# Step sizes of a state-space scan made block by block, long steps halved, and the engines' order planned anew

## The reference

```python
delta = softplus(dtl @ W_dt.T + b_dt + b_dt)            # step sizes, 512 channels
x = silu(conv(x) + conv_b)
def step(state, inp):                                    # over 512 tokens
    u, dlt, Bs, Cs = inp
    dA = exp(dlt.reshape(b, NC, DPG)[..., None] * A_g)   # 16 states for each channel
    state = dA * state + (dlt * u).reshape(b, NC, DPG)[..., None] * Bs[:, :, None, :]
    return state, einsum("bgdn,bgn->bgd", state, Cs)
y = (ys + x * D_param) * silu(z)
return y @ W_out.T
```

## Time and profile before

| | us |
|---|---|
| Time, median of 3 runs | 1946.99 |
| Lowest and highest run | 1944.04 and 1947.22 |
| The profiled execution, its own time | 1944.15 |
| Its span, first to last instruction | 1942.4 |

### The profile page before, as it was taken

One profiled execution on the slowest core, in us unless ns is written; L12 is line 12 of the kernel. 1 busy time (PEld: TensorE's weight loads), 2 busy tenths in 40 slices (PEclk: granted clock), 3 DMA queues, 4 the chain that ended last, 5 costly groups with the idle time before them and its releaser, 6 DMA issues. The chain is left out here.

```text
span 1942.4 us, 22619 instructions
## 1 busy us (share of the span) xinstructions
PE 1609.7 (83%) x5868; PEld 716.1 (37%) x5948; DVE 1521.5 (78%) x2808; ACT 1198.9 (62%) x2035; POOL 1000.3 (52%) x772
## 2 busy tenths in 40 slices
PE   2266488878997899979998899889997999789856
PEld 0113123323452346333552345234633354235224
DVE  5384599979998898969897998889986878586920
ACT  4347765677669575857577766957685536743421
POOL 0100645594449544764459444964477445864720
PEclk9987689879998899979998999989997899799988
DMA  4010022322223222322232222322232223232300
GB/s 117 2 48 22 25 85 95 111 80 79 92 92 110 73 85 77 121 77 75 87 107 81 87 88 85 115 73 90 71 121 77 82 92 119 75 111 93 123 1 11
DMA packets 94601, 157.95 MB, mean 81 GB/s; under 512 B 10940, under 2 KB 23660, under 8 KB 94468
## 3 DMA queue, kind: packets, MB, share of 16 engines
q1 hardware_dynamic: 94468, 156.43, 24.4%
HBM read 143.83 MB, written 12.58 MB: 81 GB/s over the span
## 5 line engine op out<-in xcount | busy, mean ns | idle before, releaser
L1401 POOL TENSOR_TENSOR prod<-state,c_all 128x512 f32<-128x512 f32 x512 | 653.0, 1280 | 550.5 <-DVE state L1378 436.1
L1378 DVE TENSOR_TENSOR_SCAN state<-decay,ps_b 128x512 f32<-128x512 f32 x512 | 621.8, 1214 | 53.3 <-ACT decay L1121 30.2
L924 PE MATMUL ps_y<-prod,idf 128*128 128x512 f32 x1024 | 606.2, 685 | 18.2 <-DVE u L1391 9.7
L1121 ACT ACTIVATE decay<-delta,a_neg 128x512 f32<-128x512 f32 x512 | 362.7, 721 | 222.6 <-DVE state L1378 221.9
L1385 DVE TENSOR_TENSOR ps_b<-du,ps_b 128x512 f32<-128x512 f32 x512 | 349.1, 682 | 87.2 <-PE ps_b L917 86.4
L917 PE MATMUL ps_b<-b_rows,sel_b 48*128 48x512 bf16 x512 | 207.3, 408 | 74.5 <-DVE state L1378 72.7
L924 PEld LDWEIGHTS ps_y<-prod,idf 128*128 128x128 f32 x1024 | 174.3, 203 | 165.1 <-issue 107.3
L917 PEld LDWEIGHTS ps_b<-b_rows,sel_b 48*128 48x128 bf16 x512 | 47.1, 93 | 376.5 <-DVE state L1378 234.0
L793 PE MATMUL ps_x<-xT,w 128*128 128x512 bf16 (+1 forms) x386 | 130.4, 417 | 30.7 <-DVE arena_l L1284 12.0
L896 PE MATMUL ps_x<-arena_b,fcT 128*128 128x512 f32 x256 | 125.4, 613 | 6.2 <-ACT arena_b L1103 5.5
L709 PE MATMUL ps_x<-hT,win 128*128 128x512 bf16 (+1 forms) x449 | 114.5, 388 | 13.3 <-DVE arena_b L1350 6.8
(11 more groups left out here) (236 smaller groups left out, 2411.1 us busy)
## 6 DMA issues: line engine op xcount, KB each, us to landing
c_all<-c_rows SPq DMA_DIRECT2D x512, 256.0 KB
c_rows<-arena_l SPq DMA_DIRECT2D x32, 256.0 KB
out<-arena_b SPq DMA_DIRECT2D x8, 512.0 KB
x_in<-in_base SPq DMA_DIRECT2D x8, 256.0 KB
c_all<-in_winT SPq DMA_DIRECT2D x1, 1280.0 KB, 7.1
arena_b<-in_w_fc SPq DMA_DIRECT2D x1, 1024.0 KB, 5.8
arena_b<-in_w_proj SPq DMA_DIRECT2D x1, 1024.0 KB, 4.7
w<-in_w1T SPq DMA_DIRECT2D x1, 792.0 KB, 5.8
```

The lines of the kernel that those rows point to most:

```text
L924: nc.tensor.matmul(ps_y[:], idf[:], prod[:, n % NP, :], start=(n % NST == 0), stop=(n % NST == NST - 1)).then_inc(reduced, 1)
L1121: nc.scalar.activation(decay[:, n % NDA, :], delta[:, slot(s, ct), :], ACT.Exp, scale=a_neg[:, ct, st:st + 1]).then_inc(decayed, 1)
L1378: nc.vector.tensor_tensor_scan(state[:, n % NS, :], decay[:, n % NDA, :], ps_b[:, n % NDB, :], 0.0, ALU.mult, ALU.add).then_inc(scanned, 1)
L1401: nc.gpsimd.tensor_tensor(prod[:, n % NP, :], state[:, n % NS, :], c_all[:, n % NC, :], ALU.mult).then_inc(multiplied, 1)
```

## The change

Four things are changed, and nothing of what is computed.

1. **Step sizes block by block.** The blocks are taken in the order 0, 3, 1, 2 (D_ORDER; D_AT is a block's place in it), and each block's chain of nine rounds follows the one before it, instead of the four overlapping. Block 3 has a second place and need not wait for the scan; blocks 0, 1 and 2 wait until the scan has left theirs.
2. **Long steps as two halves.** proj, gram, fc, wout, x4, apply, add and gate_root each become two steps (`halved`), so that `weave` may put something between the halves. On PE and ACT the same instructions are issued; on POOL the two additions and gate_root are issued as two instructions of half the size.
3. **The planner's tables.** BUSY and SCAN_BUSY have other numbers, and `weave` now keeps track of which activation table ACT holds and charges 128 for a change; before, the price was part of d_exp, d_log and gate_log.
4. **URGENT** has other weights, with which the order comes out anew.

```diff
+D_ORDER = (0, CT - 1) + tuple(range(1, CT - 1))
+D_AT = tuple(D_ORDER.index(i) for i in range(CT))
...
-    d0 = (14, 15, 17, 18)
     for i in range(CT):
-        k = d0[i]
+        k = 15 + 9 * D_AT[i]
         steps += [(k, "P", ("d", i)), (k + 1, "A", ("d_abs", i)), (k + 2, "A", ("d_exp", i)), (k + 3, "A", ("d_one", i)),
...
+FIRST_HALF = {"proj": "proj_a", "gram": "gram_a", "fc": "fc_a", "wout": "wout_a", "x4": "x4_a", "apply": "apply_a", "add": "add_a",
+              "gate_root": "gate_root_a"}
+def first_half(e, step):
+    if isinstance(step, str):
+        return FIRST_HALF.get(step)
+    name, i = step
+    if name in FIRST_HALF:
+        return FIRST_HALF[name], i
+    return (name, FIRST_HALF[i]) if e in "AG" and i in FIRST_HALF else None
+def halved(rounds):
+    return [[(e, part) for e, step in rnd for part in (first_half(e, step), step) if part is not None] for rnd in rounds]
+EARLY, LATE, BACK, QUANT, GATE = (halved(r) for r in (early_rounds(), late_rounds(), back_rounds(), quant_rounds(), gate_rounds()))
...
-    "A": {"apply": 196, "probs": 110, "v_relu": 110, "wo_relu": 110, "round": 30, "d_one": 52, "d_less": 52, "f_turned": 48, "p_out": 37, "relu": 48, "square": 52, "w_out": 48, "z_tanh": 49, "cw_turned": 48,
...
+    "A": {"b_turned": 91, "back apply_a": 98, "back apply": 98, "c_out": 48, "cw_turned": 48, "d_abs": 114, "d_exp": 54, "d_less": 61,
+          "d_log": 54, "d_one": 52, "dt_out": 48, "eps16": 19, "exp": 122, "f_turned": 48, "gate_abs": 17,
...
-SCAN_BUSY = {"decay": 62, "spread": 33, "drive": 60, "scan": 114, "product": 125, "sum": 87, "taken": 66, "load": 6}
+SCAN_BUSY = {"decay": 62, "spread": 33, "drive": 60, "scan": 114, "product": 123, "pair": 122, "sum": 96, "taken": 66, "load": 6}
+TABLE_LOAD = 128
+LOG_TABLE = ("log",)
+USES = {"d_log": "log", "gate_log": "log", "d_exp": "exp", "gate_exp": "exp", "exp": "exp", "decay": "exp",
+        "tanh": "tanh", "x_tanh": "tanh", "z_tanh": "tanh"}
...
-URGENT = {"late": (0.32, 0.21, 0.17, 1.42, 0.34, 0.61, 0.01, 0.02),
...
+URGENT = {"late": (1.07, 0.00728, 16.8, 1.59, 10.8, 0.0792, 0.106, 0.0435),
...
+            uses = USES.get(name_of(st[3])) if e == "A" else None
+            if uses is not None and uses not in table:
+                when, table = when + TABLE_LOAD, LOG_TABLE if uses == "log" else ("exp", "tanh")
...
-                if i < 3:
-                    eng.wait_ge(late["V"], la(s, "V", ("u", i + 1)))
-                else:
-                    eng.wait_ge(late["A"], la(s, "A", ("d_abs", 0)))
-                ins = nc.tensor.matmul(ps_x[:, D_BANK[i], :], wdt[:, i * P:(i + 1) * P], dtl, start=True, stop=True)
+                if D_AT[i] == 0:
+                    eng.wait_ge(late["V"], la(s, "V", ("u", CT - 1)))
+                elif D_AT[i] == 3:
+                    eng.wait_ge(late["A"], la(s, "A", ("d_abs", D_ORDER[0])))
+                ins = nc.tensor.matmul(ps_x[:, D_BANK[D_AT[i]], :], wdt[:, i * P:(i + 1) * P], dtl, start=True, stop=True)
...
-            elif name == "proj":
-                eng.wait_ge(back["A"], bk(s, "A", ("square", FM - 1) if i == 0 else ("p_out", i - 1)))
-                for m in range(FM):
+            elif name in ("fc_a", "fc"):
+                if name == "fc_a":
+                    if i == 0 and is_seq(s, 0):
+                        eng.wait_ge(quant["A"], 4)
+                    eng.wait_ge(back["A"], bk(s, "A", ("f_turned", 1) if i == 0 else ("relu", i - 1)))
+                k = 0 if name == "fc_a" else 1
+                ins = nc.tensor.matmul(ps_x[:, XB, :], fcT[:, k, i * P:(i + 1) * P], x3T[:, k, :],
+                                       start=(k == 0), stop=(k == KD - 1))
+            elif name in ("proj_a", "proj"):
+                if name == "proj_a":
+                    eng.wait_ge(back["A"], bk(s, "A", ("square", FM - 1) if i == 0 else ("p_out", i - 1)))
+                for m in range(0, FM // 2) if name == "proj_a" else range(FM // 2, FM):
                     ins = nc.tensor.matmul(ps_x[:, XB, 0:D], hf[:, m, i * P:(i + 1) * P], pjT[:, m, :],
                                            start=(m == 0), stop=(m == FM - 1))
...
-                ins = tt(x3, x2[:, s.par], tn, ALU.add)
+                h = slice(0, NT // 2) if i == "add_a" else slice(NT // 2, NT)
+                eng.wait_ge(back["A"], bk(s, "A", ("w", "apply_a" if i == "add_a" else "apply")))
+                if i == "add_a":
+                    wait(eng, out_stored, s.count(PER, 0))
+                ins = tt(x3[:, h], x2[:, s.par, h], tn[:, h], ALU.add)
```

128 lines of the change are left out of this document (66 added, 62 removed).

## The result

The changed kernel takes 1982.02 us (median of four runs, 1975.63 to 1983.73) where the kernel before took 1947.11 in runs beside it: 1.0174 of it, 95% interval 1.0151 to 1.0197. It is **1.7% slower**. The forecast was 1917, the range 1880 to 1946. The profiled execution took 1983.73, its span is 1981.9, which is 39.5 us more than before. It is the slowest of the four, while the profiled execution of the kernel before lies under its median, so that the spans differ by more than the medians (34.9).

The account below looks back on a forecast made before the run. DVE was taken to bound steps 0 to 7, PE steps 8 to 39, neither the loose back: 1944.15 - 18.5 (iterations 1 to 5) - 6 + 0 - 2 - 2 + 1 = 1916.65, so 1917 us, range 1880 to 1946.

Parts of the forecast that it names:

- The back of iterations 1 to 5: Steps 40 to the next iteration's start: bunches gone with step sizes block by block, 56.0 us where 70.7 were, -14.7 each.
- The front: Steps 0 to 39 of iterations 1 to 5: lengthened by work moved in, with PE nearly full, +12 us each.
- the lower bound: Front of iterations 1 to 5 were DVE the bound: about 7 us taken in less 8.9 slack, so no growth.
- The clock: PE's clock in iterations 1 to 5: with the bunches gone, half of 10 us given back, -5 (-10 to 0).
- Iteration 0: Front 3 to 5 us longer, growing with DVE alone; back about 10 shorter; together -6 (-12 to 0).
- The prologue: Before iteration 0: four more table loads, mostly covered, and gate_root behind one more POOL operation, +1 us (0 to +5).
- Iterations 6 and 7: Iteration 6: front longer, back shorter by as much, 0 us (-8 to +8); iteration 7: halves help, -2 (-6 to +1).
- Tail: End of the kernel: halved additions w.add and o.add on POOL can start earlier, -2 us.
- (c): Front packed past what in-order lists bear: it grows by 22 us, not 12; 1977 in all; chance 0.12 (over 1950).
- (a): PE's busy time overstates it and DVE bounds the front, which grows by 4, not 12; 1872, chance 0.23 (under 1900).
- (d): Order on the chip not as planned, wrong places cost what bunches did; 1938 to 1947, chance 0.15 together with (b).
- (b): Clock falls in the pure scan ending each iteration, 2 to 6 us in each of five; 1942, chance 0.15 with (d).

Follow-up runs that it names:

- the fine wait: Changed kernel, same order, with d of block 0 waiting on PE for u of block 1 again instead of the last u: 1953.89 us, 1.0024.
- the early chain ahead: The kernel with the fine wait, with sequence 1's early chain laid over the first 95% of the prologue's slots instead of all: 1940.71 us in one execution.
- the four kernels with this list: Same list in iterations 1 to 5: the fine wait, 1953.89 us; plus the early chain ahead, 1940.71; or iteration 0's last d ahead of its last sums, 1950.04; all three, 1939.68.

## Why the prediction was wrong

**The back of iterations 1 to 5: right in size, and in this order for the reasons given.** Forecast 56.0 (-14.7), measured 56.8 in iteration 4 (-13.9) and 57.8 on average (-13.6). No stall behind decay is left (DVE's waits for it fall from 30.2 to 0.4 us in the whole kernel), the last sum is still late. That only chains one behind another can do this is not shown: the run with overlapping chains has no such stalls either, and loses most of the time at the handover.

**The front: the size right once one wait is away, its reason not.** Forecast +12, measured +16.4. With the fine wait the front of iteration 4 is 150.7, +12.8. But the prediction's step "PE's busy time in steps 8 to 39 is whole, so I take a value near the upper end" does not stand: in the changed kernel 8.6 us less on PE gain 0.4, in the kernel before 10.8 less gain 4.7. DVE took in 11.0 us in steps 0 to 39 (from 128.7 to 139.7, fine wait), not the 7 of the lower bound; less its slack of 8.9 that makes +2 and not +12.8, so that DVE's work alone does not give the number either. That +12 came so near is, as far as is shown, luck. DVE's added busy time is in part not work but waiting inside its instructions, some 4 us in a whole iteration (last section).

**The missing term: a wait that the change made coarser.** It stood in the diff, u of the last block for u of the second, and the prediction put it at nothing: it did not ask what is queued behind d on PE (z, the transpose, the spread of step 40) and who waits for that (DVE's drive). It cost 2.1 to 3.6 us in steps 32 to 39 of each of iterations 1 to 5, 14.8 together, and with what goes along with it 18.9. It alone turns iterations 1 to 5 from 6.7 us faster into 12.2 slower.

**The clock: too hopeful.** Forecast -5 in iterations 1 to 5. PE spent 103.4 us of them at half rate before and 86.8 after: instead of a stretch of 17 us at the end of iterations 2, 3 and 5 there are several of 3.4 and 6.8; one of 3.4 begins at step 39 in iterations 2, 4 and 5, 0.7 to 1.4 us behind the end of PE's wait for u. In iteration 4 itself the front's clock fell from 1.00 to 0.95 (steps 0 to 7) and 0.99.

**Iteration 0: the sign wrong.** Forecast -6, from a front 3 to 5 longer and a back 10 shorter. Measured +10.5: the front took 11.0 more, the rest 0.5 less. In the rest, steps 40 to 62 gave the 9 us, and the handover took them back, 20.4 us where 11.6 were: in this order the last two blocks' chains both come at the end, one behind the other, and the second begins behind the last sums. The prediction took the back of iterations 1 to 5 for iteration 0 and did not read the new order at its end. Of the front, 5.5 are gone in the run with the fine wait, which had half the time at half rate there; in other executions of the same list it took 126.7 to 130.5 us, so this part varies with the clock.

**The prologue: a term mis-sized by 17.** Forecast +1, measured +17.7. It counted the four table loads (they are there, 13 for 9) and one POOL operation ahead of gate_root, where two stand, waiting 12.44 us for ACT. It took the interleaving as given, though the prologue's order comes from shares of slots, and the 24 added rounds push everything else of that list. Putting the early chain ahead takes 9.6 of it back; the kernel with the fine wait is 2.2 lower.

**Iterations 6 and 7: within their ranges** (-3.3 and -1.1). Iteration 6 has the long stretch that was forecast, 57.5 us for steps 8 to 15. **Tail:** +3.5 for -2; PE was at half rate for 37.9 us of it and for 27.2 before. With the fine wait it is 91.7 at 28.9 us of half rate, as before the change: the +3.5 go with the clock, and the 2 us that the halves were to save are not seen.

**The rivals.** (c) came nearest in time, 1977, but not by its mechanism: it wanted the front longer by 22 and nothing in the prologue. (a), the front held by DVE, is not it: the front did not grow by 4, and DVE's own work grew nearly as much as PE's (11.0 and 13.1 us, fine wait). (d) is out, since the back came out as planned. (b) is seen at a small scale: 6.8 us at half rate from 1285.2 on, in the thin steps around 52 of iteration 4, ahead of a wait of 2.4 us for the spread of step 54.

One reading of the prediction was off without effect: by the earlier trace rows DVE is busy for 55.0 us in steps 40 to 63 and the handover, not for 57.0.

## What to carry to other kernels

When a change reorders work, read each wait in the diff by what now stands behind it on that engine, even where the wait only names a later step of the same chain: one such word cost iterations 1 to 5 18.9 us where the new order without it gave 6.7. And an engine that is busy for 99% of a stretch is its bound only if the stretch gets shorter when its work does; on PE that takes a run to know, and where several lists are near full the work moved in has to be counted on each of them. A planned loop says nothing of the prologue and the first iteration, which have orders of their own and have to be read for themselves.

## What the runs showed of the hardware

**Less work on PE, more time at half rate.** With 12 us less matmul work in the front, PE was at half rate for 84.0 us of iterations 1 to 5 instead of 63.6 (51.7 to 66.4 in the four kernels with this list); the same edits in the kernel before gave 140.6 instead of 103.4. In steps 8 to 39 of iteration 4 the granted clock was 0.97 instead of 1.00.

**DVE beside POOL.** The DVE operations that scale the attention's norm took the same time each in the kernel before, and one in four took nearly five times that in the changed one (shortest, median and longest in ns, iterations 1 to 5, before and after):

```profile
L1156 DVE TENSOR_SCALAR arena_e<-arena_e,ri_a x20: 277/281/290, 557.3 to 1403.4; 128x256 bf16<-128x256 bf16 x20
```

```profile
L1205 DVE TENSOR_SCALAR arena_e<-arena_e,ri_a x20: 259/273/1341, 562.6 to 1413.6; 128x256 bf16<-128x256 bf16 x20
```

A POOL product takes 1.28 us. Each of the five long ones (1327 to 1341 ns) began 0.01 to 0.02 us behind the start of a POOL product (L1450) and ended 0.08 to 0.09 us behind its end; in the kernel before none of the twenty ran beside a POOL operation. A DVE operation of 128x4 elements (ve_h) took 1060 ns on average, 153 before. Such cases stood in the kernel before too, in other groups, but there are more in the new order, and DVE's busy time in iterations 1 to 5 rose by 20.7 us (918.9 to 939.6) at the same number of instructions. The Trainium skill (Advanced Engine Details and Errata, "VectorE Performance Modes") says that VectorE's second port is shared with GpSimd and that the two block each other in the two-port modes; the trace agrees, 273 ns alone and 1341 at worst. The time counts as busy, so that a busy DVE, too, is not all work.
